# Even and odd attention heads on the two 64-row halves of TensorE's array

## The reference

```python
x = L0_attn_x                                    # (2, 1024, 128)
q = (xn @ Wq.T + bq).reshape(b, n, 16, 8)...     # xn = layernorm(x); k, v alike
sim = einsum('bhid,bhjd->bhij', q, k) + bias*SCALE + causal
out = einsum('bhij,bhjd->bhid', softmax(sim), v)
x = x + out @ Wo.T + bo
h = relu(layernorm(x) @ w1[0] + b1[0]);  t = layernorm(x)
x = x + layernorm(t + h @ w2[0] + b2[0]) * gamma + beta
```

## Time and profile before

| | us |
|---|---|
| median of 3 runs (365.61 to 368.34) | 368.16 |
| the profiled execution | 367.01 |
| its span | 365.2 |
| TensorE busy in the span | 326.3 (89%) |
| VectorE busy | 273.8 (75%) |
| ScalarE busy | 190.4 (52%) |
| GpSimd busy | 65.5 (18%) |
| mean granted clock of TensorE | 0.946 |

### The profile page before, as it was taken

How to read it: one execution, slowest core, us unless ns; L and a number is a source line. 1 busy time by engine, 2 the same in 40 slices (tenths; PEclk the granted TensorE clock), 3 DMA queues, 4 the chain that set the end, 5 groups by cost and what they waited for, 6 DMA issues and landing times.

```text
span 365.2 us, 8215 instructions
## 1 busy us (share of the span) xinstructions
PE 326.3 (89%) x3233; PEld 155.1 (42%) x3235; DVE 273.8 (75%) x952; ACT 190.4 (52%) x262; POOL 65.5 (18%) x79
## 2 busy tenths in 40 slices
PE   8846886699999998998999999899999989999971
PEld 4323442242444354344434434444443443348741
DVE  5565374985777895887799589689969987547895
ACT  1340595134557536655754665574466557763330
POOL 4118999300000000000000000000000001432551
PEclk9985698957999999999999999999999999999997
DMA  7455317200202201020220123032112102000022
GB/s 203 138 176 134 82 46 242 82 4 1 66 2 66 61 9 46 24 66 1 68 63 7 52 48 93 2 90 73 31 55 48 24 3 39 9 2 16 0 57 58
DMA packets 13830, 20.89 MB, mean 57 GB/s; under 512 B 2944, under 2 KB 10240, under 8 KB 13664
## 3 DMA queue, kind: packets, MB, share of 16 engines
q1 hardware_dynamic: 13104, 17.28, 17.4%
q10 hardware_dynamic: 688, 3.09, 3.1%
HBM read 13.90 MB, written 4.23 MB: 50 GB/s over the span
## 4 chain that ended last, share of the span: by engine, by line
PE 58%; DVE 16%; ACT 14%; issue 5%; POOL 3%; DMA 2%; ACTq 1%; DVEq 0%; POOLq 0%
PE ps L1029 15%; PE ps L1072 15%; PE ps L1043 14%; ACT PT L647 10%; PE ps L1060 6%; DVE FM L783 4%; DVE junk L790 3%; PE ps L963 2%; ACT TT L605 2%; POOL XN L495 2%; PE ps L1105 2%; DVE st L858 1%; DVE U L911 1%; DMA qk_scratch<-QS 1%; DMA table_s<-in_table 1%
## 5 line engine op out<-in xcount | busy, mean ns | idle before, releaser
L647 ACT ACTIVATE PT<-ps 128x1024 f32<-128x1024 f32 (+1 forms) x192 | 145.6, 810 | 113.0 <-PE ps L1060 95.0
L783 DVE TENSOR_REDUCE FM<-ps 128x1 f32<-128x512 f32 (+3 forms) x176 | 108.2, 660 | 18.3 <-PE ps L1029 18.2
L790 DVE CUSTOM_DVE_ANT_0 junk<-ps,NBH 128x256 bf16<-128x256 f32 (+1 forms) x256 | 89.5, 403 | 33.9 <-PE ps L1029 33.7
L1029 PE MATMUL ps<-KA,QA 72*128 72x256 bf16 (+3 forms) x544 | 107.2, 291 | 2.2 <-DVE FM L783 1.0
L1043 PE MATMUL ps<-QA,KA 74*128 74x512 bf16 (+3 forms) x384 | 95.7, 334 | 11.1 <-ACT PT L647 9.7
L1072 PE MATMUL ps<-PT,VG 128*16 128x512 f32 (+3 forms) x768 | 86.9, 498 | 0.0
L1029 PEld LDWEIGHTS ps<-KA,QA 72*128 72x128 bf16 x544 | 43.9, 100 | 87.2 <-DVE FM L783 33.1
L541 POOL TENSOR_SCALAR tmp<-mv 128x4 f32<-128x4 f32 x8 | 2.3, 289 | 266.5 <-DVE mv L861 266.5
L1043 PEld LDWEIGHTS ps<-QA,KA 74*128 74x128 bf16 x384 | 31.9, 99 | 36.8 <-ACT PT L647 24.0
L1060 PE MATMUL ps<-TT,flb 128*32 128x176 f16 (+4 forms) x1152 | 38.5, 243 | 0.0
L1060 PEld LDWEIGHTS ps<-TT,flb 128*32 128x32 bf16 x1152 | 21.3, 96 | 17.5 <-issue 16.6
(11 more groups left out here) (93 smaller groups left out, 250.1 us busy)
## 6 DMA issues: line engine op xcount, KB each, us to landing
QA<-qk_scratch SPq DMA_DIRECT2D x48, 96.0 KB
KA<-qk_scratch SPq DMA_DIRECT2D x42, 96.0 KB
qk_scratch<-QS SPq DMA_DIRECT2D x8, 384.0 KB, 4.1
X<-in_x SPq DMA_DIRECT2D x4, 256.0 KB, 5.3
PT<-fr_scratch ACTq DMA_DIRECT2D x1, 1024.0 KB, 4.6
out<-U SPq DMA_DIRECT2D x4, 256.0 KB, 2.3
OT<-f_scratch ACTq DMA_DIRECT2D x2, 480.0 KB, 8.7
xnT<-OT SPq DMA_DIRECT2D x28, 32.0 KB
```

The costliest lines, as they stand in the source:

```text
L647: nc.scalar.activation(PT[:, s % 3, 2 * q:2 * q + 2, off:off + w], ST[:, q, :, off:off + w], ACT.Exp).then_inc(s_exp, 1)
L783: nc.vector.tensor_reduce(FM[:, ib, heads[0]:heads[-1] + 1, piece], bank[:, 0:w * len(heads)].rearrange("p (h n) -> p h n", n=w), AX.X, AL ...
L790: last = nc.vector.tensor_tensor_reduce(junk[:, k % NSM, i, 0:w], bank[:, i * w:(i + 1) * w], nb[:, h, 256 - w:256], 1.0, NEG, ALU.add, AL ...
L1029: last = nc.tensor.matmul(bank[:, i * w + j - j0:i * w + j - j0 + n], QA[0:KS, p, ib // 4, h, (ib % 4) * 128:(ib % 4 + 1) * 128], KA[0:KS, ...
```

## The change

Heads 0 and 2 of a group go to array rows 0 to 63, heads 1 and 3 to rows 64 to 127. `QA` and `KA` hold eight of the nine products (64 rows) for each half, two heads deep; `QB` and `KB` hold the ninth product and the two maximum rows (10 rows at 0 and at 64). A score is two products, 64 rows and then 10, which add up in the same bank; the maximum pass uses the 64-row product alone. A far unit holds only heads of one parity, so there are 42 units; TensorE issues them as jobs, an even unit and the odd one behind it, alternating between the two row halves and banks, after a wait for both banks. A half of the keys and queries is loaded by 16 DMAs instead of 6, the maxima are moved by two instead of one. The first user of the second half is now job 12, again in step 5 after the second scores; the second "m" is in step 0 after the values. The placing functions, the wait counts, the buffers of the feed-forward layer and the order of the heads in the weights are adapted.

```diff
-KS = ROWS
-KST = MROW + 2
+HP = HG // 2
+KS = 64
+KLOW = HD + 2
...
-                nh = min(HG, 512 // pw)
-                for h0 in range(0, HG, nh):
-                    out.append(("far", ib, list(range(h0, h0 + nh)), j0, pw, piece))
-        nh = HG if ib == 0 else 2
-        for h0 in range(0, HG, nh):
-            out.append(("near", ib, list(range(h0, h0 + nh))))
+                nh = min(HP, 512 // pw)
+                for q0 in range(0, HP, nh):
+                    for e in range(2):
+                        out.append(("far", ib, [2 * q + e for q in range(q0, q0 + nh)], j0, pw, piece))
+        for e in range(2):
+            out.append(("near", ib, [2 * q + e for q in range(HP)]))
...
+JOBS = [k for k in range(NU) if UNITS[k][0] == "m" or UNITS[k][2][0] % 2 == 0]
...
-        QA = sb("QA", [128, 2, 2, HG, IC], BF16)
-        KA = sb("KA", [128, 2, 2, HG, IC], BF16)
+        QA = sb("QA", [128, 2, 2, HP, IC], BF16)
+        KA = sb("KA", [128, 2, 2, HP, IC], BF16)
+        QB = sb("QB", [128, 2, 2, HP, IC], BF16)
+        KB = sb("KB", [128, 2, 2, HP, IC], BF16)
...
         def load_q(eng, g, p, c):
 
-            for u in range(NPART):
-                eng.dma_start(QA[u * NPART * HD:(u + 1) * NPART * HD, p, c, :, :].rearrange("r h n -> r (h n)"),
-                              bass.AP(qk_d, g * GN + 2 * c * NPART * PN, [[HG * IC, HD], [PN, NPART], [1, HG * IC]])
+            at = g * GN + 2 * c * NPART * PN
+            for e in range(2):
+                for u in range(2):
+                    r0 = 64 * e + 24 * u
+                    eng.dma_start(QA[r0:r0 + 24, p, c, :, :].rearrange("r h n -> r (h n)"),
+                                  bass.AP(qk_d, at + e * HP * IC, [[HG * IC, HD], [PN, NPART], [1, HP * IC]])
+                                  ).then_inc(s_ldqk[p][c], 16)
+                eng.dma_start(QA[64 * e + 48:64 * e + 64, p, c, :, :].rearrange("r h n -> r (h n)"),
+                              bass.AP(qk_d, at + e * HP * IC, [[HG * IC, HD], [PN, 2], [1, HP * IC]])
                               ).then_inc(s_ldqk[p][c], 16)
+            for e in range(2):
+                eng.dma_start(QB[64 * e:64 * e + HD, p, c, :, :].rearrange("r h n -> r (h n)"),
+                              bass.AP(qk_d, at + 2 * PN + e * HP * IC, [[HG * IC, HD], [1, HP * IC]])
+                              ).then_inc(s_ldqk[p][c], 16)
...
-                sp.dma_start(QA[MROW:MROW + 2, p, half, :, :], mrow[:, half, :]).then_inc(s_md[half], 16)
+                for e in range(2):
+                    r0 = 64 * e + HD
+                    sp.dma_start(QB[r0:r0 + 2, p, half, :, :],
+                                 mrow[4 * e:4 * e + 4, half, :]).then_inc(s_md[half], 16)
...
-                nc.gpsimd.memset(KA[64:KST, p, :, :, :].rearrange("p c h n -> p (c h n)"), 1.0).then_inc(s_zero, 1)
+                nc.gpsimd.memset(KB[:, p, :, :, :].rearrange("p c h n -> p (c h n)"), 1.0).then_inc(s_zero, 1)
...
-                for i, h in enumerate(heads):
-                    for j, n in cuts:
-                        last = nc.tensor.matmul(bank[:, i * w + j - j0:i * w + j - j0 + n],
-                                                QA[0:KS, p, ib // 4, h, (ib % 4) * 128:(ib % 4 + 1) * 128],
-                                                KA[0:KS, p, j // IC, h, j % IC:j % IC + n], start=True, stop=True)
-                last.then_inc(s_smr, 1)
+                pieces = [(i, h // 2, j, n) for i, h in enumerate(u[2]) for j, n in cuts]
+                pe.wait_ge(s_smf, NU * g + k + 2)
+                for m, (i, q, j, n) in enumerate(pieces):
+                    for e in range(2):
+                        last = nc.tensor.matmul(SM[:, (k + e) % NSM, i * w + j - j0:i * w + j - j0 + n],
+                                                QA[64 * e:64 * e + KS, p, ib // 4, q, (ib % 4) * 128:(ib % 4 + 1) * 128],
+                                                KA[64 * e:64 * e + KS, p, j // IC, q, j % IC:j % IC + n],
+                                                start=True, stop=True)
+                        if m == len(pieces) - 1:
+                            last.then_inc(s_smr, 1)
...
-                    pe.wait_ge(s_md[ic], 16 * g + 16)
+                    pe.wait_ge(s_md[ic], 32 * g + 32)
...
-                for h in range(2 * q, 2 * q + 2):
-                    last = nc.tensor.matmul(ST[:, q, h % 2, off:off + w],
-                                            KA[0:KST, p, jb // 4, h, (jb % 4) * 128:(jb % 4 + 1) * 128],
-                                            QA[0:KST, p, ic, h, off:off + w], start=True, stop=not near,
+                for e in range(2):
+                    nc.tensor.matmul(ST[:, q, e, off:off + w],
+                                     KA[64 * e:64 * e + KS, p, jb // 4, q, (jb % 4) * 128:(jb % 4 + 1) * 128],
+                                     QA[64 * e:64 * e + KS, p, ic, q, off:off + w], start=True, stop=False,
+                                     skip_group_check=True)
+                for e in range(2):
+                    last = nc.tensor.matmul(ST[:, q, e, off:off + w],
+                                            KB[64 * e:64 * e + KLOW, p, jb // 4, q, (jb % 4) * 128:(jb % 4 + 1) * 128],
+                                            QB[64 * e:64 * e + KLOW, p, ic, q, off:off + w], start=False, stop=not near,
                                             skip_group_check=True)
...
-                                pe.wait_ge(s_ldqk[1 - p][HALF_UNITS[k]], 96 * load)
-                            unit(g + 1, 1 - p, k)
+                                pe.wait_ge(s_ldqk[1 - p][HALF_UNITS[k]], LOADED * load)
+                            job(g + 1, 1 - p, k)
```

More of the change, by code:

```diff
@@ L131, in places @@
     costs = [unit_cost(u) for u in UNITS]
-    out, own, done = {}, {}, 0.0
-    for u in range(NU):
-        at = t * (S_START + (S_END - S_START) * done / sum(costs[:-1]))
+    out, own = {}, {}
+    for u in JOBS:
+        at = t * (S_START + (S_END - S_START) * sum(costs[:u]) / sum(costs[:-1]))
         if u == NU - 1:
             at = t * M1_AT
-        done += costs[u]
         s, pos = next((s, pos) for c, s, pos in pts if c > at % t)
@@ L157, in places0 @@
     slots = [(s, pos) for s in range(FIRST_STEP[1] - 1) for pos in range(3)]
-    for u in range(OWN0 + 2, NU - 1):
-        own.setdefault(slots[(u - OWN0 - 2) * len(slots) // (NU - 3 - OWN0)], []).append(u)
+    for u in JOBS:
+        if OWN0 + 4 <= u < NU - 1:
+            own.setdefault(slots[(u - OWN0 - 4) * len(slots) // (NU - 5 - OWN0)], []).append(u)
     own[slots[-1]].append(NU - 1)
-    out[slots[-1]] = list(range(FIRST0))
+    out[slots[-1]] = [u for u in JOBS if u < FIRST0]
     slots = [(s, pos) for s in range(FIRST_STEP[1] - 1, NSTEP) for pos in range(3)]
-    for u in range(FIRST0, NEXT0):
-        out.setdefault(slots[(u - FIRST0) * len(slots) // (NEXT0 - FIRST0)], []).append(u)
+    for u in JOBS:
+        if FIRST0 <= u < NEXT0:
+            out.setdefault(slots[(u - FIRST0) * len(slots) // (NEXT0 - FIRST0)], []).append(u)
     return out, own
@@ L266, in build, with hidden @@
         tT = work[:, 10 * IC:12 * IC].rearrange("p (c n) -> p c n", c=2)
-        hid = [work[:, 0:4 * IC],
-               KA[:, 0:1, :, :, :].rearrange("p o c h n -> p (o c h n)").bitcast(F32)]
+        hid = [work[:, 0:4 * IC]] + [
+            a[:, 0:1, :, :, :].rearrange("p o c h n -> p (o c h n)").bitcast(F32) for a in (QA, KA)]
+        def hidden(c, f):
+            if c % 2 == 0:
+                return hid[0][:, f * IC:(f + 1) * IC]
+            return hid[1 + f // 2][:, (f % 2) * IC:(f % 2 + 1) * IC]
         R = [PT[:, 1, :, :], OT[:, 4:6, :].rearrange("p g (c n) -> p (g c) n", n=IC)]
@@ L798, in unit @@
                     nm = NM[:, half, :]
-                    m0, m1 = (MC[:, half, :, q, :] for q in range(2))
+                    m0, m1 = (MC[:, half, :, :, q, :] for q in range(2))
                     v = 4 * g + 2 * half
@@ L1007, in _, with job @@
                 task_flip(i)
-            def unit(g, p, k):
+            def job(g, p, k):
                 u = UNITS[k]
-                bank = SM[:, k % NSM, :]
-                pe.wait_ge(s_smf, NU * g + k + 1)
                 if u[0] == "m":
-                    half = u[1]
+                    bank, half = SM[:, k % NSM, :], u[1]
+                    pe.wait_ge(s_smf, NU * g + k + 1)
                     pe.wait_ge(s_ms, 2 * g + half + 1)
@@ L1119, in task @@
                             pe.wait_ge(e_hs, h_count(TASKS2.index((f"h{f}", c))))
-                        last = nc.tensor.matmul(tile_of(i), hid[c % 2][:, f * IC + i * 128:f * IC + (i + 1) * 128],
+                        last = nc.tensor.matmul(tile_of(i), hidden(c, f)[:, i * 128:(i + 1) * 128],
                                                 w2_s[:, f, :], start=(f == 0), stop=(f == 3), skip_group_check=True)
@@ L1127, in s_units_at @@
                     for k in (OWN_UNITS0 if first else OWN_UNITS).get((s, pos), []):
```

(8 more changed lines are left out.)

45 lines of the change are left out of this document (27 added, 18 removed).

## The result

The changed kernel takes 433.57 us (median of 4 runs, 430.38 to 436.05), the kernel before 367.13 (365.61 to 368.34): a ratio of 1.181, 95% interval 1.170 to 1.192. Slower was forecast, at 428 us. The profiled execution of the kernel after is the slowest of its four.

A forecast was written before the change was run, and what follows sets the result against it. TensorE's stream was taken as the bound, with SyncE's DMA issue to overtake its cover. 3.4 + 5.8 + 6 x (5.0 + 3.0) + 3.0 = 60.2 us on 367.0 gave 427, as median 428 us; range 396 to 460.

The forecast's parts named there:

- start and group 0: Program start: extra K-load issues on ScalarE cost 3.4 us, then SyncE's longer queue up to the scores 5.8 us.
- stretch A: Second-half maxima's transposes to the new half's first product: 15.0 us instead of 10.00, 5.0 more in groups 1 to 6.
- clock: TensorE's granted clock falls after a 3.6 us gap in each of six groups: 3.0 us a group, bounds 0 and 6.8.
- stretch C: Rest of the period, new half's first product to next transposes: stays 21.75 us, paired savings against changes and weight loads.
- last group: Last group: no maximum pass, 36 more changes, partly under other waits, cost 3.0 us (0 to 5).
- SyncE's issue: SyncE's queue behind the transposes: 18 DMAs at 0.69 us each, path 15.0 us, while TensorE needs the data at 11.4.
- Rival 3: SyncE's loads stay hidden, at 0.42 us a DMA or less, and the pairs' saving remains: 351 us; chance 0.08.
- rival 4: SyncE's issue is cheap but TensorE's changes cost: 33.15 us a group, about 379 us; chance 0.06.
- Pairs and changes: TensorE: paired row halves overlap fully, maximum pass 3.84 us a group less; each change between 64-row and 10-row products costs 0.10.
- Rival 1: TensorE: the clock holds, 410 us, or row-tile changes are free with a clock price of 1.7, 402 us; chance 0.20.
- 2 (no overlap): TensorE's pairs do not overlap: scores +7.68 us a group, maximum pass gains nothing, 459 us; chance 0.10.
- VectorE stays hidden: VectorE, with two more, smaller reductions a group, is busy 26.1 us and adds nothing to TensorE's 33.1.

The follow-up runs named there:

- warm: The kernel after, with 16 idle TensorE products of 512 columns on zeros ahead of each wait for the second half: 418.38 us, 1.138.
- b16: The kernel before with only its loads cut, 16 DMAs a half instead of 6 and two for the maximum rows: 416.02 us, 1.129.
- poolk: The kernel after with the K loads of groups 2 to 7 issued by GpSimd instead of SyncE: 402.83 us, 1.096.
- rows64: The kernel after with the second score product on 64 rows, 54 of them zeros: 410.66 us, 1.117.
- start: poolk plus rows64, separate bank waits, first and group 1's K loads on GpSimd, group 1's last Q load behind the stores: 379.29 us, 1.034.
- dvehalf: The kernel of start with about half of VectorE's maximum pass left out, so maxima of fewer columns: 359.06 us, 0.976.

## Why the prediction was right, and which terms were off

The direction, the place and the mechanism held. The terms, in us of the span, by the prediction's own steps:

| step | predicted | measured | from |
|---|---|---|---|
| start and group 0 | 3.4 + 5.8 = 9.2 | 13.4 | second transposes of group 1's maxima at 121.82, before 108.4 |
| stretch A, six groups | 6 x 5.0 = 30.0 | 24.4 | 14.19 in the period shown against 10.00 |
| clock, six groups | 6 x 3.0 = 18.0 | 17.2 | stretches C, 159.7 against 142.6 in warm |
| stretch C without the stalls' clock, six groups | 0 | 11.1 | 142.6 in warm against 131.5 before |
| last group | 3.0 | 2.9 | last transposes to the end, 68.3 against 65.3 |
| sum | 60.2 | 69.0 | |

*SyncE's issue* was the step that carried the forecast, and b16 and poolk show it. It was a little too dear: the 24-row and 16-row loads took 0.66 to 0.70 us each, as read from the earlier trace rows (but for one pair at 0.96), the four 8-row loads only 0.40 each, and TensorE started 1.3 us after the last issue, not 1.7. Rival 3, the hidden loads, would have needed 0.42 us for all of them; rival 4 needed a cheap issue too and fell with it.

*Pairs and changes* held. Pairs overlap in full; a change between 64 and 10 rows costs the 0.10 us carried over from the earlier trace rows. So rivals 1 (free changes) and 2 (no overlap) fell, by the timeline and by rows64. Rival 1's other half, a clock that holds, fell too: the clock fell at each of the six stalls.

*The step that failed* is stretch C: "The new rule that a job waits for two free banks leaves one unit of 0.62 us queued, longer than a pair; nothing", with it "VectorE stays hidden", and the 1.1 us of idle time "that the longer scores fill". TensorE's own work came to less than forecast, 20.6 us busy for 21.75. But it waited: 1.4 us for VectorE and still 1.2 us for ScalarE in the stretch C of warm, together 2.6 us where the sum has none. So C grew by 1.6 us at full clock, and by 3.1 in the sixth group, at whose end warm ran at 1.2 GHz too. In a kernel without stalls the wait for VectorE takes the whole gain of the pairs: 2.55 us a group between start and dvehalf. The reason is argued from the code and not shown. In the kernel before a unit waits for the bank of three units ago; VectorE then has up to two units in hand. A job needs the bank of two units ago for its second half and then gives VectorE two units at once, followed by a stretch without any. A run with four banks would test it.

*The start* was 4.2 us too cheap in this execution. In warm, the same program up to there, the mark was reached at 118.85, 3.0 us earlier (in poolk at 118.86); by that the start came out 1.2 us above the forecast. ScalarE's extra issues cost 2.9 us (TensorE's product behind the `NBH` copies starts at 27.80, before at 24.92), near the 3.4; but the first transposes came 5.95 us late (54.24, before 48.29), with 2.16 us of idle time behind VectorE just ahead of them, where before there were 0.56. SyncE's `move_m` was issued at 85.51 instead of the predicted 82.7, and the scores behind it started at 88.02, 11.5 us later than before. The other 1.9 us came behind that, and the prediction had "no more" clock there: TensorE was at 1.2 GHz for 13.0 us from these scores on (to 101.0), before for 10.1. By my estimate, half of the difference, that is 1.4 us.

The forecast of 428 came out near 433.6 partly by luck: A was forecast 5.6 us too dear and C 11.1 too cheap, and these and the start partly cancel.

Left open: what part of VectorE's wait in the kernel after is the two banks and what part the placement of the jobs, since dvehalf was run on the mended kernel only; and why equal stalls are followed by low clock of such different length. A layout that loads a 64-row half in fewer DMAs wasn't tried.

## What to carry to other kernels

Count DMAs, not bytes, wherever loads stand in order behind an event: cutting 6 loads into 16 with the same bytes cost an eighth of the time, because one queue issued them in a gap of 10 us. Before two units are joined into one job, look at how many buffers remain for the consumer: an engine at 80% of the period can take back all that the producer saves, while its share of busy time says that it has room. And a stall can cost twice, once as idle time and once as slow clock behind it; where it can't be removed, products on zeros can fill it.

## What the runs showed of the hardware that I had not expected

- An issue on SyncE's queue does not cost the same for all small loads: 0.40 us for a load of 8 rows with one run of addresses a row, 0.66 to 0.70 for 16 and 24 rows gathered from two or three planes. GpSimd's issue of such loads took 0.55 to 0.60 us each, 8-row ones among them.
- With some hundred DMAs issued by GpSimd the end of the program, behind VectorE's last instructions, was 4.2 us longer (96 loads) and 6.2 us longer (120); with one such DMA it was as before.
- After an idle gap of 3.3 us TensorE ran for 9 us at 1.2 GHz, though it was busy for nearly all of it. Behind gaps of nearly the same length the low clock lasted 3.4 us in rows64 and between 3.4 and 10.2 us in b16. Products on zeros in the gap kept it at 2.4 GHz.
- Between products of 64 and of 10 rows 0.10 us is lost at each change, while 54 more rows of zeros, which make both 64, cost nothing.
